# A two-layer attention kernel with every engine's order rewritten: small products set between long projections, group moments in three VectorE operations instead of two

## The chip, the cores and the metric

The kernel runs on one core of a Trainium2 chip. The metric is the device time of one execution in microseconds (us). The comparison is between the kernel before and the kernel with the change, each timed in several runs; one further execution of each is recorded by the hardware profiler.

## The reference

The input is 32 images of 16 x 16 positions with 256 channels, all float32. Two residual layers follow each other, each behind a group normalisation with 32 groups of 8 channels. Layer 0 is windowed attention (8 x 8 windows, shifted by 4, 16 heads, cosine similarity, a position bias, softmax). Layer 1 is linear attention along the columns and along the rows (no softmax), the two results added.

```python
def _gn(v, G=32, eps=1e-05):
    g = v.reshape(B_, H_, W_, G, C_ // G)
    m = jnp.mean(g, axis=(1, 2, 4), keepdims=True)
    s = jnp.var(g, axis=(1, 2, 4), keepdims=True)
    return ((g - m) / jnp.sqrt(s + eps)).reshape(v.shape)
# layer 0, on windows xw of the shifted image
q, k, v = xw @ Wq.T, xw @ Wk.T, xw @ Wv.T + bv
logits = (q / |q|) . (k / |k|) * scale + 16 * sigmoid(bias) + mask
z = softmax(logits) . v @ Wo.T + bo
# layer 1, for the columns and for the rows
q, k, v = split(x @ w_qkv, 3)
out = (q . k^T * d ** -0.5) . v @ w_out
x = x + layer0(_gn(x)); x = x + layer1(_gn(x))
```

## The kernel before, in words

**Work.** An image is held with channels on the 128 partitions, as two halves of 256 tokens. Each operand of a large product is split into a float16 high part and a float16 low part (the remainder), and a product takes three passes (PASSES). So each tensor that feeds TensorE costs a copy to float16 on ScalarE (`..._high`) and a subtraction for the remainder, on GpSimd (`..._low`: whole minus high, line L908) or on VectorE where the whole lies in PSUM.

**Staging.** The kernel is written by hand as five instruction streams, one per engine, and each stream is a loop over steps k. In step k a stream works on several images, each at another stage: `for img in there(k - 3): axial_kv(1, img)` means that in step k the row half of layer 1 makes keys and values of image k - 3. In full swing each step does all of the work of one image, so the length of a step times 32, and the ramps at both ends, is the time. Within a step the order is written out by hand; each engine runs its stream strictly in that order and waits on semaphores: `reach(engine, semaphore, img)` waits until that stage of that image is done (`earlier(img, 2)` is two images back, `earlier(img, -1)` one ahead); `edge(...)` is the same wait, written only for the first and the last 8 images.

**TensorE**, by stage: `window_qk` (24 products of 256 columns), `window_v` (12), `scores` (96 small ones), `window_pv` (64 small), `window_den` (16), `window_out` (12); `group_means` (a product of 12 columns that spreads the group sums, once per layer); `axial_kv` (12 of 512 columns, for a = 0 columns and a = 1 rows), `axial_q` (12), `gram_matmuls` (96 small), `axial_out` (32 pairs of small ones), `axial_y` (24), and transposes `image_channels`, `result_rows`.

**The chain that matters.** On VectorE `add_x` adds the residual, `group_stats` takes statistics of each half, `group_moments` turns them into mean and second moment (four numbers a partition), TensorE's `group_means` sums over the group, `group_var` makes the variance in four tiny operations, GpSimd's `rstd` raises to the power -0.5 (L913), and `group_norm` applies it. `gn_small[layer]` counts the tiny steps, GN_STEPS per image. On VectorE also: `cap_norms`, `spread_norms`, `scale_qk` (the query and key norms), `mask_k`, `add_bias` (two operations of 1024 elements, behind `scores`), `gram_low`, `q1_low`, `o1_sum`, and `turn_squares` and `sum_heads` behind ScalarE's `squares`. The lines in the profile are L1050 and L1052 for the moments, L1059 to L1066 for the variance, L1188 for `add_x`, L1098 for `o1_sum`.

**DMA.** Products of layer 1 are spread over partitions by DMAs from SyncE's queue (`spread_v_rows`, `spread_gram`).

**PSUM banks** are fixed per stage (QK_BANK and so on), so a stage that writes a bank waits for the reader of the stage that had it before.

## Time and profile before

| | us |
|---|---|
| three runs of the kernel before, median (lowest to highest) | 1011.24 (1006.41 to 1012.84) |
| profiled execution, device time | 1005.87 |
| its span in the profile | 1004.1 |
| TensorE busy (share of the span) | 862.2 (86%) |
| VectorE busy | 757.0 (75%) |
| ScalarE busy | 663.8 (66%) |
| GpSimd busy | 494.9 (49%) |
| mean granted TensorE clock, share of full | 0.963 |

The profiled execution lies 5.4 us under the median of the three runs. Busy time of TensorE counts overlapping small products once. L12 is line 12 of the kernel file, PE is TensorE (matmul), DVE is VectorE, ACT is ScalarE, POOL is GpSimd.

### The profile page before, as it was taken

To read this page: it belongs to the slowest core of one execution; us is meant where nothing else is said; L and a number is where in the kernel's file an instruction comes from. 1 tells how busy PE (TensorE), PEld (TensorE's weight loads), DVE (VectorE), ACT (ScalarE), POOL (GpSimd) and SP (SyncE) were. 2 spreads that over 40 slices of the span, in tenths; PEclk is the share of its full clock that TensorE was granted. 3 is DMA by queue.
4 is the path that set the end of the run, shared out by engine and by line. 5 is a ranking of instruction groups with operands and counts; after the bars stand their busy time and mean duration, and the time that the engine had idled before them with its cause. 6 is when DMAs were issued, how large, how long until landed. Compare 5 with 4: busy or idle time off the path is not lost.

```text
span 1004.1 us, 45923 instructions
## 1 busy us (share of the span) xinstructions
PE 862.2 (86%) x20128; PEld 662.0 (66%) x20128; DVE 757.0 (75%) x1493; ACT 663.8 (66%) x1106; POOL 494.9 (49%) x361
## 2 busy tenths in 40 slices
PE   2257899999999999889999989999999998999765
PEld 2244676777777776667777767777777776767554
DVE  3666888889888877788887777898888877797321
ACT  2336676777777777777666767777777776777441
POOL 5125455655555554645555546555555545544431
PEclk9777999999999999999999999999999999999887
DMA  5100333343333434343333343433333443333333
GB/s 167 32 12 17 73 75 72 72 86 72 69 78 71 79 79 85 80 85 67 71 71 74 78 84 80 86 73 71 74 78 73 83 83 80 74 66 66 65 76 74
DMA packets 334158, 74.04 MB, mean 74 GB/s; under 512 B 282356, under 2 KB 333446, under 8 KB 333958
## 3 DMA queue, kind: packets, MB, share of 16 engines
q1 hardware_dynamic: 333958, 71.11, 34.4%
q8 instruction: 158, 2.59, 1.1%
q14 instruction: 42, 0.34, 0.1%
HBM read 12.31 MB, written 8.40 MB: 21 GB/s over the span
## 4 chain that ended last, share of the span: by engine, by line
PE 55%; DVE 17%; issue 10%; ACT 9%; SPq 4%; POOL 2%; DMA 2%; ACTq 0%; POOLq 0%; DVEq 0%
PE ps L546 17%; PE ps L454 15%; DVE stat L1052 5%; PE ps L577 5%; ACT kv L717 3%; PE ps L592 3%; SPq L404 3%; PE ps L511 3%; PE ps L502 3%; DVE o L1098 3%; ACT v_diag L801 2%; PE ps L477 2%; PE ps L593 2%; PE ps L617 2%; PE ps L493 2%
## 5 line engine op out<-in xcount | busy, mean ns | idle before, releaser
L908 POOL TENSOR_TENSOR kv<-kv,kv 128x1024 f16<-128x1024 f32 x64 | 137.1, 2142 | 136.1 <-ACT kv L717 136.1
L908 POOL TENSOR_TENSOR xn<-xn,xn 128x512 f16<-128x512 f32 x64 | 74.4, 1162 | 122.4 <-ACT xn L754 122.4
L592 PE MATMUL ps<-q,gram_wide 128*128 128x32 f16 x2048 | 111.3, 176 | 6.1 <-DMA gram_wide<-gram 5.2
L577 PE MATMUL ps<-v_wide,kv 64*32 64x128 f16 x6144 | 73.8, 226 | 47.9 <-DVE o L1098 27.2
L1105 DVE STREAM_TRANSPOSE qk<-qk_sq 128x1024 f32<-128x1024 f32 x32 | 39.9, 1246 | 98.7 <-ACT qk_sq L772 98.7
L592 PEld LDWEIGHTS ps<-q,gram_wide 128*128 128x128 f16 x2048 | 108.7, 97 | 8.0 <-DMA gram_wide<-gram 5.8
L593 PE MATMUL ps<-q,gram_wide 128*128 128x16 f16 x2048 | 110.5, 169 | 0.0
L734 ACT ACTIVATE gram<-ps,small 128x512 f16<-128x512 f32 x128 | 94.8, 810 | 22.4 <-PE ps L577 22.4
L1092 DVE SCALAR_TENSOR_TENSOR gram<-ps,small,gram 128x512 f16<-128x512 f32 x128 | 93.5, 784 | 17.8 <-ACT gram L734 15.9
L593 PEld LDWEIGHTS ps<-q,gram_wide 128*128 128x128 f16 x2048 | 106.1, 97 | 0.7
L454 PE MATMUL ps<-xn,w_q 128*128 128x256 f16 x768 | 97.1, 276 | 6.8 <-POOL xn L908 4.5
L722 ACT ACTIVATE kv<-ps 128x1024 f32<-128x1024 f32 x64 | 65.5, 1024 | 53.8 <-PE ps L546 53.8
L577 PEld LDWEIGHTS ps<-v_wide,kv 64*32 64x32 f16 x6144 | 61.3, 91 | 55.9 <-issue 42.6
L604 PE MATMUL ps<-o,w_o 128*128 128x256 f16 x768 | 92.9, 280 | 3.2 <-POOL o L908 3.2
L546 PE MATMUL ps<-w_kv,xn_cols 128*128 128x512 f16 x384 | 92.1, 390 | 1.3 <-issue 1.1
L913 POOL TENSOR_TENSOR stat<-stat,small 128x2 f32<-128x2 f32 x64 | 52.0, 812 | 80.5 <-DVE stat L1066 79.3
L908 POOL TENSOR_TENSOR xn_cols<-xn,xn_cols 128x512 f16<-128x512 f32 x32 | 45.2, 1411 | 90.3 <-ACT xn_cols L760 90.3
L546 PE MATMUL ps<-w_kv,xn 128*128 128x512 f16 x384 | 89.0, 382 | 0.3 <-POOL xn L908 0.3
L604 PEld LDWEIGHTS ps<-o,w_o 128*128 128x128 f16 x768 | 76.9, 100 | 14.6 <-POOL o L908 4.0
L908 POOL TENSOR_TENSOR o<-o,o 128x512 f16<-128x512 f32 x64 | 74.3, 1161 | 23.2 <-ACT o L748 23.2
L908 POOL TENSOR_TENSOR qk<-qk 128x1024 f16<-128x1024 f32 x32 | 68.7, 2148 | 30.6 <-ACT qk L787 30.6
L454 PEld LDWEIGHTS ps<-xn,w_q 128*128 128x128 f16 x768 | 70.6, 99 | 19.2 <-issue 7.3
(119 smaller groups left out, 2003.2 us busy)
## 6 DMA issues: line engine op xcount, KB each, us to landing
gram_wide<-gram SPq DMA_DIRECT2D x256, 128.0 KB
v_wide<-kv SPq DMA_DIRECT2D x512, 32.0 KB, 2.0
x_in<-x SPq DMA_DIRECT2D x32, 128.0 KB
x_in<-x SPq DMA_DIRECT2D x64, 64.0 KB
out<-y_out SPq DMA_DIRECT2D x32, 128.0 KB
out<-y_out SPq DMA_DIRECT2D x64, 64.0 KB
probs<-L_conv_w_qkv SPq DMA_DIRECT2D x1, 768.0 KB, 4.9
x<-L_conv_w_qkv SPq DMA_DIRECT2D x1, 768.0 KB, 6.5
```

The lines of the kernel that those rows point to most:

```text
L454: last = pe.matmul(dst, w[:, wp, c, m * P:m * P + P], act[:, xp, c * TOK:(c + 1) * TOK], start=(n == 0), stop=(n == 5))
L546: last = pe.matmul(ps[:, KV_BANK[a] + t, :], xn1[a][:, xp, c * TOK + t * P:c * TOK + t * P + P], w_l1[a]["kv"][:, wp, c, :], start=(n == 0 ...
L577: last = pe.matmul(dst.rearrange("p (s e) -> p s e", e=32), kv[a][rows, kp, t, own], v_wide[a][rows, :, vp, t, own], start=(n == 0), stop= ...
L592: pe.matmul(dst.rearrange("p (t i) -> p t i", t=2), high, q1[a][:, :, cols], start=True, stop=False)
L593: last = pe.matmul(dst[:, 0:SEQ], low, q1[a][:, 0, cols], start=False, stop=True)
L604: last = pe.matmul(ps[:, Y_BANK, g * TOK:(g + 1) * TOK], w_l1[a]["o"][:, wp, c2, g * P:(g + 1) * P], o1[a][:, xp, c2 * TOK:(c2 + 1) * TOK] ...
L722: act.activation(kv32[a][:], ps[:, KV_BANK[a]:KV_BANK[a] + 2, :], ACT.Copy).then_inc(kv_copied[a], 1)
L734: last = act.activation(gram_half(a, head, 0), gram_psum(a, head), ACT.Copy, scale=gram_mask[:, head:head + 1])
L908: return pool.tensor_tensor(dst, whole, high, ALU.subtract)
L913: pool.tensor_tensor(stat[layer][:, 28:30], stat[layer][:, 26:28], minus_half, ALU.pow).then_inc(gn_pow[layer], 1)
L1052: dve.scalar_tensor_tensor(sq_sum, sq_sum, 2.0 / TOK, s[:, 12:16], ALU.mult, ALU.add).then_inc(done, 1)
L1092: last = dve.scalar_tensor_tensor(gram_half(a, head, 1), gram_psum(a, head), gram_mask[:, head:head + 1], gram_half(a, head, 0), ALU.mult, ...
```

## The change

All five streams get a new order, every PSUM bank is assigned anew, the waits follow from that, and some stages move to another step (TensorE's stream has 38 steps in place of 37). In `group_moments` the one operation that scaled the second moment and added the squared mean becomes a multiplication by a constant and an addition; GN_STEPS goes from 10 to 11. No product, copy or DMA is added or dropped.

```diff
-        GN_STEPS = 10
+        GN_STEPS = 11
...
-        QK_BANK, V_BANK, DEN_BANK, PV_BANK, Z_BANK, Y_BANK, YT_BANK, XT_BANK = 4, 7, 4, 3, 3, 3, 2, 2
-        S_BANK, KV_BANK, Q_BANK = (5, 3), (5, 6), (5, 2)
-        G_BANK, O_BANK, GM_BANK = (0, 0), (0, 3), (7, 2)
+        QK_BANK, V_BANK, DEN_BANK, PV_BANK, Z_BANK, Y_BANK, YT_BANK, XT_BANK = 6, 7, 1, 5, 0, 0, 0, 5
+        S_BANK, KV_BANK, Q_BANK = (2, 5), (1, 1), (7, 4)
+        G_BANK, O_BANK, GM_BANK = (3, 3), (5, 2), (1, 0)
...
             def scores(img):
-                reach(pe, o1_summed[1], earlier(img, 3))
-                edge(pe, k_masked, img)
+                reach(pe, o1_summed[0], earlier(img, 3))
+                edge(pe, kv_hi[1], earlier(img, 2))
...
             def axial_out(a, img):
                 reach(pe, gram_spread[a], img, 64)
                 if a == 0:
-                    edge(pe, gram_lo[1], img)
+                    reach(pe, xt_copied, earlier(img, -4))
                 else:
-                    reach(pe, y_added, earlier(img, 1))
+                    reach(pe, biased[0], earlier(img, -3))
+                    edge(pe, kv_hi[1], earlier(img, -1))
...
             def group_means(layer, img):
+                reach(pe, gn_small[layer], img, GN_STEPS, 5)
                 if layer == 0:
-                    reach(pe, v_ready, earlier(img, 1))
-                    edge(pe, gn_small[0], img, GN_STEPS, 4)
-                else:
-                    reach(pe, xt_copied, earlier(img, -2))
-                    reach(pe, gn_small[1], img, GN_STEPS, 4)
+                    reach(pe, kv_hi[1], earlier(img, 3))
...
             def group_moments(layer, img):
                 reach(dve, done, img, GN_STEPS, 2)
                 dve.tensor_tensor(s[:, 12:16], mean, mean, ALU.mult).then_inc(done, 1)
-                reach(dve, done, img, GN_STEPS, 3)
-                dve.scalar_tensor_tensor(sq_sum, sq_sum, 2.0 / TOK, s[:, 12:16], ALU.mult, ALU.add).then_inc(done, 1)
+                dve.tensor_scalar(sq_sum, sq_sum, 2.0 / TOK, None, ALU.mult).then_inc(done, 1)
+                reach(dve, done, img, GN_STEPS, 4)
+                dve.tensor_tensor(sq_sum, sq_sum, s[:, 12:16], ALU.add).then_inc(done, 1)
```

A whole step of TensorE's stream now reads: `window_v`, `group_means(1)`, `axial_out(0)`, `axial_q(1)`, `axial_q(0)`, `group_means(0)`, `scores`, `axial_y`, `axial_out(1)`, `window_pv`, `window_den`, `window_qk`, `result_rows`, `gram_matmuls(0)`, `axial_kv(0)`, `window_out`, `image_channels`, `gram_matmuls(1)`, `axial_kv(1)`.

The rows below are instructions in the order in which an engine runs them, with what each writes and reads, sizes, and a count of equal ones.

TensorE before, in the middle of the program, from the rows' gram products to the queries and keys of layer 0 (`kv` with `v_wide` is `gram_matmuls`, `qk` with `k_two` is `scores`):

```order
L577 MATMUL ps<-v_wide,kv 32x128 x96
L477 MATMUL ps<-w_v,xn 128x256 x12
L493 MATMUL ps<-qk,k_two 128x64 x96
L454 MATMUL ps<-xn,w_q 128x256 x12
L639 MATMUL ps<-stat,group 128x12
L577 MATMUL ps<-v_wide,kv 32x128 x96
L546 MATMUL ps<-w_kv,xn_cols 128x512 x12
L502 MATMUL ps<-probs,small 32x256 x8
L617 MATMUL ps<-ident,y 128x128 x4
L511 MATMUL ps<-probs,v_diag 32x64 x32
```

TensorE after, from the queries and keys of layer 0 to the group sum of layer 1 of the next step:

```order
L454 MATMUL ps<-xn,w_q 128x256 x12
L454 MATMUL ps<-xn,w_k 128x256 x12
L620 MATMUL ps<-ident,y 128x128 x4
L580 MATMUL ps<-v_wide,kv 32x128 x96
L548 MATMUL ps<-w_kv,xn_cols 128x512 x12
L454 MATMUL ps<-o,w_o 128x256 x12
L630 MATMUL ps<-ident,x_in 128x128 x4
L580 MATMUL ps<-v_wide,kv 32x128 x96
L548 MATMUL ps<-w_kv,xn 128x512 x12
L477 MATMUL ps<-w_v,xn 128x256 x12
L638 MATMUL ps<-stat,group 128x12
```

Three groups of small products stood within five rows; now each gram group has a long projection behind it, and layer 1's group sum stands right behind the values of layer 0.

VectorE before, behind the sum over heads; `x1` is the residual sum of layer 1's input:

```order
L1112 TENSOR_REDUCE head_sum<-qk32 128x64
L1188 TENSOR_TENSOR x1<-z,x_t 128x32x8 x2
L1123 SCALAR_TENSOR_TENSOR head_norm<-head_rnorm,head_scale 128x64
L1043 BN_STATS stat1<-x1 128x6 x2
L1129 STREAM_TRANSPOSE qk_sq<-head_norm 128x1024
L1050 TENSOR_TENSOR stat1<-stat1 128x4
L1052 SCALAR_TENSOR_TENSOR stat1<-stat1 128x4
L1135 TENSOR_TENSOR qk32<-qk_sq,ps 128x1024
```

VectorE after, at the same place:

```order
L1114 TENSOR_REDUCE head_sum<-qk32 128x64
L1094 SCALAR_TENSOR_TENSOR gram<-ps,small,gram 128x32x16 x2
L1125 SCALAR_TENSOR_TENSOR head_norm<-head_rnorm,head_scale 128x64
L1131 STREAM_TRANSPOSE qk_sq<-head_norm 128x1024
L1137 TENSOR_TENSOR qk32<-qk_sq,ps 128x1024
L1190 TENSOR_TENSOR x1<-z,x_t 128x32x8 x2
L1044 BN_STATS stat1<-x1 128x6 x2
L1051 TENSOR_TENSOR stat1<-stat1 128x4
L1052 TENSOR_SCALAR stat1<-stat1 128x4
L1054 TENSOR_TENSOR stat1<-stat1 128x4
L1094 SCALAR_TENSOR_TENSOR gram<-ps,small,gram 128x32x16 x2
```

The residual sum and the moments of layer 1 stood ahead of the scaling of queries and keys, and now stand behind it and behind one `gram_low`.

GpSimd before, the remainders around the normed queries and keys (`qk`):

```order
L908 TENSOR_TENSOR o<-o32,o 128x512
L908 TENSOR_TENSOR kv_0<-kv32_0,kv_0 128x1024
L908 TENSOR_TENSOR o1_1<-o1_32_1,o1_1 128x512
L908 TENSOR_TENSOR kv_1<-kv32_1,kv_1 128x1024
L908 TENSOR_TENSOR qk<-qk32,qk 128x2x512
L913 TENSOR_TENSOR stat1<-stat1,small 128x2
```

GpSimd after:

```order
L909 TENSOR_TENSOR o<-o32,o 128x512
L909 TENSOR_TENSOR kv_0<-kv32_0,kv_0 128x1024
L909 TENSOR_TENSOR o1_0<-o1_32_0,o1_0 128x512
L909 TENSOR_TENSOR qk<-qk32,qk 128x2x512
L909 TENSOR_TENSOR o1_1<-o1_32_1,o1_1 128x512
L914 TENSOR_TENSOR stat1<-stat1,small 128x2
L909 TENSOR_TENSOR kv_1<-kv32_1,kv_1 128x1024
L914 TENSOR_TENSOR stat0<-stat0,small 128x2
```

Both `o1` remainders now stand directly around that of `qk`, and the remainder of `kv_1` moved from ahead of the power of layer 1 to between the two powers.

## Rows read from the trace of the kernel before

**Rows 1.** The page, parts 1 and 2: busy time, and the granted clock

```profile
PE 862.2 (86%) x20128; PEld 662.0 (66%) x20128; DVE 757.0 (75%) x1493; ACT 663.8 (66%) x1106; POOL 494.9 (49%) x361
...
PEclk9777999999999999999999999999999999999887
```

**Rows 2.** The chain that ended last, columns' keys and values (start, length, what)

```profile
161.42 2.70 PE ps L546 x12
...
868.96 2.70 PE ps L546 x12
```

**Rows 3.** The same chain from 640 to 675 us

```profile
642.43 0.95 PE ps L577 x96
643.38 2.70 PE ps L546 x12
...
647.08 0.59 PE ps L617 x4
...
648.69 2.73 PE ps L454 x24
...
653.01 1.33 PE ps L454 x12
```

**Rows 4.** Waits, longest in total: who waited for whom, us, times, longest

```profile
PE ps L577 <- DVE o L1098: 27.2, 28, 1.1
...
PE ps L639 <- ACT v_diag L801: 11.1, 16, 2.0
...
PE ps L577 <- issue: 10.9, 14, 1.2
PE ps L493 <- issue: 9.8, 13, 1.0
```

**Rows 5.** VectorE in order of time, from 517.5 us

```profile
517.85 0.26 DVE L1050 TENSOR_TENSOR stat<-stat 128x4 f32<-128x4 f32 x1
518.14 2.07 DVE L1052 SCALAR_TENSOR_TENSOR stat<-stat 128x4 f32<-128x4 f32 x1
...
521.98 0.87 DVE L1145 TENSOR_SCALAR k_two<-qk,small 128x1024 f16<-128x1024 f16 x2
```

**Rows 6.** GpSimd in the same stretch

```profile
515.95 2.14 POOL L908 TENSOR_TENSOR kv<-kv,kv 128x1024 f16<-128x1024 f32 x1 [4.35 <-ACT kv L717]
518.04 2.15 POOL L908 TENSOR_TENSOR qk<-qk 128x1024 f16<-128x1024 f32 x1
521.56 0.94 POOL L913 TENSOR_TENSOR stat<-stat,small 128x2 f32<-128x2 f32 x1 [1.36 <-DVE stat L1066]
```

**Rows 7.** VectorE from 67 us, then TensorE from 66 us

```profile
70.56 0.16 DVE L1062 TENSOR_TENSOR stat<-stat 128x2 f32<-128x2 f32 x1
70.75 1.97 DVE L1064 TENSOR_TENSOR stat<-stat 128x2 f32<-128x2 f32 x1
...
73.78 1.47 PE L493 MATMUL ps<-qk,k_two 32*128 32x64 f16 x96 [3.16 <-DVE k_two L1145]
```

**Rows 8.** Groups by line: count, busy us, mean ns of one, idle before

```profile
L1092 DVE SCALAR_TENSOR_TENSOR gram<-ps,small,gram 128x512 f16<-128x512 f32 x128 | 93.5, 784 | 17.8 <-ACT gram L734 15.9
L1152 DVE TENSOR_TENSOR probs<-ps,bias_mask 128x1024 f32<-128x1024 f32 x64 | 75.2, 1218 | 5.2 <-PE ps L493 4.7
...
L1129 DVE STREAM_TRANSPOSE qk_sq<-head_norm 128x1024 f32<-128x1024 f32 x32 | 39.3, 1229 | 0.0
...
L1188 DVE TENSOR_TENSOR x<-z,x_t 128x256 f32<-128x256 f32 x64 | 24.4, 422 | 12.2 <-ACT z L824 12.2
```

**Rows 9.** The same view of ScalarE and of GpSimd

```profile
L717 ACT ACTIVATE kv<-ps 128x1024 f16<-128x1024 f32 x64 | 65.3, 1020 | 0.0
...
L908 POOL TENSOR_TENSOR kv<-kv,kv 128x1024 f16<-128x1024 f32 x64 | 137.1, 2142 | 136.1 <-ACT kv L717 136.1
...
L908 POOL TENSOR_TENSOR o<-o,o 128x512 f16<-128x512 f32 x64 | 74.3, 1161 | 23.2 <-ACT o L748 23.2
...
L913 POOL TENSOR_TENSOR stat<-stat,small 128x2 f32<-128x2 f32 x64 | 52.0, 812 | 80.5 <-DVE stat L1066 79.3 <-DVE stat L1064 1.2
```

More of the change, by code:

```diff
@@ L412, in step @@
             def step(k):
-                for img in there(k - 5):
+                for img in there(k - 6):
+                    spread_v_rows(0, img)
                     spread_v_rows(1, img)
@@ L643, in step @@
                 for img in there(k - 2):
+                    window_v(img)
+                for img in there(k - 3):
+                    group_means(1, img)
+                for img in there(k - 5):
+                    axial_out(0, img)
+                for img in there(k - 4):
+                    axial_q(1, img)
+                    axial_q(0, img)
+                for img in there(k - 1):
+                    group_means(0, img)
+                for img in there(k - 2):
+                    scores(img)
@@ new lines, in step @@
+                for img in there(k - 6):
+                    axial_y(img)
+                for img in there(k - 5):
+                    axial_out(1, img)
+                for img in there(k - 2):
+                    window_pv(img)
+                    window_den(img)
+                for img in there(k - 1):
+                    window_qk(img)
+                for img in there(k - 6):
+                    result_rows(img)
+                for img in there(k - 4):
+                    gram_matmuls(0, img)
@@ L651, in step @@
-                for img in there(k - 2):
-                    group_means(1, img)
-                for img in there(k - 3):
-                    axial_q(0, img)
-                for img in there(k - 4):
-                    axial_out(1, img)
-                for img in there(k - 3):
-                    gram_matmuls(0, img)
-                for img in there(k - 1):
-                    window_v(img)
-                    scores(img)
-                for img in there(k - 3):
-                    axial_q(1, img)
@@ L678, in step @@
-                for img in there(k - 3):
-                    axial_out(0, img)
-            over_steps(step, 6)
+            over_steps(step, 7)
         @block.scalar
@@ L960, in step @@
                     token_low(0, img)
-                for img in there(k - 4):
-                    o1_low(1, img)
-                for img in there(k - 2):
-                    token_low(1, img)
-            over_steps(step, 5)
+            over_steps(step, 6)
         @block.vector
@@ L1250, in step @@
                     sum_heads(img)
-                for img in there(k - 1):
-                    add_x(img)
+                for img in there(k - 3):
+                    gram_low(0, img)
             over_steps(step, 6)
```

186 lines of the change are left out of this document (90 added, 96 removed).

## The prediction

> **What bounds the kernel now.** I read the page first. TensorE is busy for 86% of the span, VectorE for 75%, the others less [rows 1]; the granted clock is at its full level (2.4 GHz) nearly everywhere between the ramps [rows 1]. So no engine is full, and the clock is not what is lost. The chain that ended last gives the length of a step: the columns' keys and values of one image begin at 161.42 us, those of the image 25 later at 868.96 us [rows 2], so a step takes (868.96 - 161.42)/25 = 28.3 us. The same chain gives what TensorE's groups cost when one follows the other: 2.70 us for twelve products of 512 columns, 1.33 for twelve of 256, 2.73 for twenty-four, 0.95 for a group of small ones, 0.59 for four transposes [rows 3]; the pairs of `axial_out` lie between 651.42 and 653.01, which is 1.6 us [rows 3].
>
> The waits tell what fills the rest. TensorE waited 28 times, 27.2 us in all, for `o1_sum` (L1098) ahead of the gram products, 16 times for the spread of v, and 14 and 13 times, 10.9 and 9.8 us, in the middle of gram and score products for nothing the profile can name ("issue") [rows 4]. The first is 0.97 us a step, the second 11.1/28 = 0.4 and the issue gaps 20.7/28 = 0.7 as means over the steps. Without them a step would take 28.3 - 0.97 - 0.4 - 0.7 = 26.2. From the other side, group by group [rows 3]: the stages of 256 columns (queries and keys 2.73, y 2.7, and v, out and two q at 1.33 to 1.4) make 10.8, keys and values 2 x 2.7 = 5.4, and the small ones (two grams, scores, spread of v, denominators at 1.0 or so each, two `axial_out` at 1.6, transposes and sums 1.3) 9.5: 25.7. I take the middle, **25.9 us**, as TensorE's floor.
>
> Why is `o1_sum` late? Ahead of it on VectorE stands L1052, an operation on four numbers a partition that takes 2.07 us [rows 5]. It ends at 520.21; GpSimd's remainder of qk, from 518.04, ends at 520.19 [rows 6]. L1050, just before it, began at 517.85 and ended at 518.11, when GpSimd's remainder of kv had ended at 518.09 [rows 5, 6]. So a VectorE operation with two SBUF inputs stands still while GpSimd subtracts, and slips through at the border between two GpSimd operations. It is not a matter of the fused form: a plain TENSOR_TENSOR on two numbers took 1.97 us in one place and 0.16 just before it [rows 7]. This **hold** is what I follow through the new order.
>
> **The change part by part.**
>
> *The moments as plain operations.* Unheld, one more tiny operation costs about 0.2 us with its semaphore, by the two operations of rows 7 (starts 0.19 apart). That is 0.4 us a step of VectorE, where it has room. The hold is not removed: the last of the three still has two SBUF inputs. For the middle one, a TENSOR_SCALAR, no row of before shows it behind a GpSimd subtraction, so its hold lies between 0 and the length of one such subtraction, 1.16 us [rows 9].
>
> The Trainium skill, in "SBUF — State Buffer", section on which operations grab the shared pair of ports, says that `tensor_scalar` can run in a mode that takes VectorE's second port too and is then blocked like the two-input form. By that rule the middle operation would be held as well, and the sum below would be the same to 0.2 us, as the third is held behind the same subtraction.
>
> *The issue gaps.* All lie inside small groups that stood three in five rows; with a long projection behind each they should go: -0.7 us a step, or nothing if they come from elsewhere. They would be hidden by the waits below in any case.
>
> The Trainium skill, in "Runtime: NRT & Kernel Launch", section on instruction fetch, holds that fetching is hidden since the sequencer dispatches slower than blocks arrive. By that the gaps are something else and stay, up to 0.7 us a step; the rows show only their place.
>
> *The wait for o1_sum.* The gram products no longer follow directly on it, -0.97 us a step; `scores` waits for it now, with one long step of distance. Gone too is the wait for the spread of v.
>
> *The new order, followed from the end of `window_qk` (time 0).* ScalarE squares (1024 elements, 1.02 as the copy of [rows 9]), VectorE turns and sums (each as long as the transposition of rows 8, 1.23) to 3.6; then one `gram_low` (2 x 0.78 overlapping, 1.4), `cap_norms` 0.2, `spread_norms` 1.23, `scale_qk` 1.2, all from [rows 8, 9] or by the like size there. `add_x` is ready to start at **7.55**. TensorE meanwhile does 0.6 + 1.0 + 2.7 and ends the columns' kv at 4.3 [rows 3]; ScalarE copies it twice, 2 x 1.02 [rows 9], to 6.3; GpSimd subtracts from 6.4 to **8.5** (2.14) [rows 9]. So the first `add_x`, two SBUF inputs, is held to 8.5 and reads on to 8.8. GpSimd's next, the remainder of o1_0, is ready and takes 8.8 to 9.95; the second `add_x` goes through at 10.2; the remainder of qk takes 10.2 to 12.35 (as in rows 6); statistics end at 11.0, the first moment operation is held to 12.35; the remainder of o1_1 runs to 13.5; the second and third moment operations end at **13.7**. Without any hold it would be 7.55 + 0.8 + 0.8 + 0.4 = 9.5.
>
> TensorE goes on from 4.15 with 1.33 + 0.45 + 1.0 + 2.6 + 1.42 and stands at `group_means(1)` at 10.95. That group sum needs the moments. Held, it starts at 13.9: **TensorE idles 2.9 us**. Unheld it would not wait (9.5 < 10.95). Behind it are queued `axial_out(0)`, both `axial_q`, `scores`, and so `add_bias`.
>
> *A second hold.* From the moments (call it M) VectorE goes through `gram_low`, statistics, `mask_k`, moments, `o1_sum`, `group_var(1)`: 1.4 + 0.7 + 0.8 + 0.4 + 0.6 + 0.7, to M + 4.4 (the shapes of [rows 5, 8], each start some 0.08 before the end of the one ahead; statistics taken as long as two `add_x`, `o1_sum` as half a `add_bias`, the variance as four of the 0.19 of rows 7). GpSimd then takes the power, 0.81 as a mean [rows 9] and 0.94 when VectorE's `k_two` overlaps it [rows 5, 6], and at M + 5.2 begins the remainder of kv_1, to M + 7.3. TensorE's group sum of layer 0 ends at M + 0.2 + 0.3 + 1.6 + 2 x 1.33 + 0.3 = M + 5.1, so the two-input operations of `group_var(0)` come at M + 5.3 to 5.5 and are held to M + 7.3. `add_bias` (2 x 1.22 [rows 8]) then ends at M + 9.9 and releases `axial_out(1)` (wait on `biased[0]`) at M + 10.0. TensorE is there at M + 4.9 + 0.95 + 2.65 = M + 8.5: **idle 1.5 us more**. The rest meets its times: the remainder of xn that `window_qk` needs comes some 0.4 us before it.
>
> *Sum.* 25.9 + 2.9 + 1.5 = 30.3 us a step, against 28.3: +2.0. Of the 38 steps some 26 are full and the others pay part; I count 27: +54 us. The ramps have one step more but an image passes 5.8 steps in place of 5.7: 0, give or take 10. Against the profiled execution, 1005.9 + 54 = **1060 us**; that execution lies 5.4 under the median of the runs, inside their spread, so the same number stands for the median.
>
> **The rivals.**
>
> *Half of the holds.* If `group_var(0)` gets through (its margin is 0.1 to 0.3 us, against a power of 0.7 or 0.95), the step is 25.9 + 2.9 = 28.8: 1005.9 + 0.5 x 27 = 1019. If the two `add_x` go through together and the middle moment is not held, the third ends at 12.4, the first idle time is 1.6 and the step 29.0: 1025; both together 27.5: 984. For: margins are small and each is read from one row. Together 985 to 1035.
>
> *No hold decides; TensorE bounds: faster.* This is the other side. If the `kv_0` subtraction ends before `add_x` comes, or `group_stats` lands in a free stretch, the moments are ready before 10.95 and the step falls to the floor, 25.9: 1005.9 - 2.4 x 27 = 941. It decides at 1.4 us of hold in all (10.95 - 9.5). For it: all other waits have slack, the issue gaps go. Against: the first overlap alone (7.55 inside 6.4 to 8.5) is 1 us long, and two more subtractions are queued right behind. 935 to 985.
>
> *The clock falls.* With 2.9 and 1.5 us of idle time a step TensorE may be granted half its clock (1.2 GHz) at times: in the ramp, where the clock row shows 7 [rows 1], the score group behind 3.16 us of idle time took 1.47 us [rows 7], where a group of 96 at full clock takes 0.95 [rows 3]. If a third of the steps ran their 8 us between the two waits so, about 3 us more each: +1 us a step, 1087; more often, 1110.
>
> *The issue gaps stay* where TensorE does not wait anyway: +0.3 a step, 1068, inside the forecast's own range.
>
> **How the numbers follow.** The forecast (both holds) 45%, own range 1035 to 1080; half of the holds 20%; TensorE-bound 20%; falling clock 12%; gaps stay 3%. The range must hold 8 in 10: from 962 (most of the TensorE-bound case left out, 17%) to 1100 (3%). Within 1% of 1011 is what a measurement of this kernel can hardly tell from no change: 1001 to 1021. Faster than that: the 20% and a quarter of the half-holds' 20%, 26%. Same: about 15%. Slower: 59%.
>
> **What would show it.** Right: the list of waits has TensorE waiting at the group sum (L638) for the last moment operation (L1054), near 2.9 us a time, and at `axial_out(1)` for `add_bias` (L1154); L1190 shows means far over 0.42 us, L1051, L1052 and L1054 over 0.2, L1064 or L1066 some 2 us in each step, each ending with a GpSimd row; issue gaps vanish from L580 and L493. Wrong: L1190 at 0.42 and the group sum unwaited. The forecast fails if a hold is not what it seems (the arbitration lets VectorE's pairs through), or if a chain through DMA (`gram_spread`, due 0.7 us before `axial_out(0)` in the TensorE-bound case) becomes the limit.

## The result, and the profile after

The changed kernel takes 1058.59 us as the median of four runs (1057.6 to 1061.35), the kernel before 1008.89 (1006.41 to 1012.84, four runs beside them, three of which are those of the table before): a ratio of 1.0516, 95% interval 1.0482 to 1.0551. The profiled execution of after has a span of 1057.1 us.

The page of after, parts 1, 2 and 4, against [rows 1, 2]:

```profile
PE 888.2 (84%) x20128; PEld 678.8 (64%) x20128; DVE 837.1 (79%) x1557; ACT 659.0 (62%) x1106; POOL 495.4 (47%) x361
...
PEclk8579889999999899999999999999999999899987
...
PE 46%; DVE 34%; issue 11%; ACT 5%; SPq 3%; DMA 1%; POOL 0%; DVEq 0%; POOLq 0%; ACTq 0%
```

The same instructions keep TensorE busy 26 us longer and VectorE 80 us longer. VectorE did not get 80 us of work: 64 small operations of 0.16 us are 10 us. Most of the rest is standing still: `add_x` (L1190) alone shows 78.2 us in place of 24.4. VectorE carries a third of the chain that ended last. The mean granted clock of the core is 0.914, before 0.963. With the two levels of 1 and 0.5 that is 2 x 0.086 x 1057.1 = 182 us at the lower level (1.2 GHz), against 2 x 0.037 x 1004.1 = 74 us before, most of that in the ramps.

The step can be read from the four transposes of `x_in`, which stand once in each. Here those of image 7 and image 31, with first and last start:

```profile
L630 PE MATMUL ps<-ident,x_in x4: 272/272/273, 209.0 to 209.3; 128*128 128x128 f32 x4
...
L630 PE MATMUL ps<-ident,x_in x4: 272/272/273, 926.4 to 926.8; 128*128 128x128 f32 x4
```

(926.4 - 209.0)/24 = **29.89 us** a step. Before, the same two stand at 202.6 and 882.3: 28.32. So the middle costs 24 x 1.57 = 38 us, the start up to image 7 another 6.4, and the end behind image 31 (130.6 us in place of 121.7) 8.9.

The waits of after (who waited for whom: us, times, longest), against [rows 4]:

```profile
PE ps L638 <- DVE stat L1054: 77.4, 35, 2.7
...
PE ps L596 <- issue: 8.1, 9, 2.7
...
PE ps L596 <- DVE probs L1154: 4.7, 11, 0.7
```

TensorE's wait for `o1_sum` is gone. In its place `group_means` waits 35 times, 2.2 us a time, for the last of the moments. The wait of `axial_out(1)` for `add_bias`, forecast at 1.5 us a step, is small: 4.7 us under that name, and in the 24 steps another 3.1 us of the L596 waits called "issue", which end 0.10 us behind the end of `add_bias` like the named ones (0.15). Together that is 0.3 us a step.

VectorE's groups by line, against [rows 8]: busy, then the mean of one in ns.

```profile
L1190 DVE TENSOR_TENSOR x<-z,x_t 128x256 f32<-128x256 f32 x64 | 78.2, 1260 | 3.6 <-ACT z L822 3.6
L1051 DVE TENSOR_TENSOR stat<-stat 128x4 f32<-128x4 f32 x64 | 41.7, 651 | 1.1
L1054 DVE TENSOR_TENSOR stat<-stat 128x4 f32<-128x4 f32 x64 | 33.9, 529 | 2.2
L1064 DVE TENSOR_TENSOR stat<-stat 128x2 f32<-128x2 f32 x64 | 29.7, 464 | 2.2
...
L1052 DVE TENSOR_SCALAR stat<-stat 128x4 f32<-128x4 f32 x64 | 10.3, 161 | 0.0
```

`add_x` (L1190) takes three times its 422 ns of before. One step in order of time shows why. `window_qk` ended at 500.13. VectorE, then GpSimd, from there on:

```profile
507.64 2.42 DVE L1190 TENSOR_TENSOR x<-z,x_t 128x256 f32<-128x256 f32 x2
...
510.89 1.18 DVE L1051 TENSOR_TENSOR stat<-stat 128x4 f32<-128x4 f32 x1
511.99 0.16 DVE L1052 TENSOR_SCALAR stat<-stat 128x4 f32<-128x4 f32 x1
512.18 1.00 DVE L1054 TENSOR_TENSOR stat<-stat 128x4 f32<-128x4 f32 x1
...
519.62 0.85 DVE L1064 TENSOR_TENSOR stat<-stat 128x2 f32<-128x2 f32 x1
...
520.82 2.36 DVE L1154 TENSOR_TENSOR probs<-ps,bias_mask 128x1024 f32<-128x1024 f32 x2
```

```profile
506.35 2.14 POOL L909 TENSOR_TENSOR kv<-kv,kv 128x1024 f16<-128x1024 f32 x1 [3.41 <-ACT kv L720]
508.44 1.34 POOL L909 TENSOR_TENSOR o<-o,o 128x512 f16<-128x512 f32 x1
509.75 2.30 POOL L909 TENSOR_TENSOR qk<-qk 128x1024 f16<-128x1024 f32 x1
512.01 1.15 POOL L909 TENSOR_TENSOR o<-o,o 128x512 f16<-128x512 f32 x1
...
518.33 2.13 POOL L909 TENSOR_TENSOR kv<-kv,kv 128x1024 f16<-128x1024 f32 x1
```

Each held operation ends with a GpSimd row: L1051 at 512.07 with qk at 512.05, L1054 at 513.18 with the second o at 513.16, L1064 at 520.47 with kv at 520.46. L1052 slips in at the border between two subtractions, as in every step: its 64 times are all 149 to 194 ns, and none had to start in the middle of a subtraction. TensorE in the same step, and what clock it was granted in four stretches (busy times and counts by engine, then the granted clock):

```profile
509.41 1.47 PE L477 MATMUL ps<-w_v,xn 128*128 128x256 f16 x12
513.24 0.39 PE L638 MATMUL ps<-stat,group 128*128 128x12 f32 x2 [2.35 <-DVE stat L1054]
```

```profile
512.00:514.50 2.50, 1.26 (x43) 1.26 (x44) 2.46 (x6) 1.17 (x4) 1.16 (x2) 1.00 0.00 0
514.50:517.90 3.40, 3.40 (x44) 2.59 (x41) 2.96 (x13) 1.51 (x2) 0.22 (x1) 0.50 0.47 81
517.90:520.00 2.10, 2.10 (x101) 1.96 (x100) 0.54 (x2) 0.60 (x1) 2.10 (x2) 0.99 0.79 143
```

TensorE is idle for 2.35 us, works on for 1.3 us, and is then at its lower level for 3.4 us. Of the 24 steps, 23 hold such a fall of the clock. The one that holds none, from 268.3 us, shows what the two holds do when TensorE keeps its speed:

```profile
281.36 2.05 DVE L1066 TENSOR_TENSOR stat<-stat 128x2 f32<-128x2 f32 x1
```

```profile
281.27 2.13 POOL L909 TENSOR_TENSOR kv<-kv,kv 128x1024 f16<-128x1024 f32 x1
```

```profile
286.01 0.18 PE L596 MATMUL ps<-q,gram_wide 128*128 128x32 f16 x1 [1.32 <-issue]
```

The group sum of layer 1 waits 2.35 us there too, the variance of layer 0 is held for 2.05 us, `add_bias` ends at 285.90, and `axial_out(1)` has waited 1.32 us when it starts 0.1 us behind that. The step takes 29.31 us.

### The profile page after: what moved, and what is told of

It reads as the page before. It is cut to its first block, busy times and chain, and to the rows that moved or that the text cites. A ratio compares the mean times of both kernels' runs of the same rounds, so it can differ in the third digit from the quotient of the medians.

```text
span 1057.1 us, 45985 instructions
## 1 busy us (share of the span) xinstructions
PE 888.2 (84%) x20128; PEld 678.8 (64%) x20128; DVE 837.1 (79%) x1557; ACT 659.0 (62%) x1106; POOL 495.4 (47%) x361
## 4 chain that ended last, share of the span: by engine, by line
PE 46%; DVE 34%; issue 11%; ACT 5%; SPq 3%; DMA 1%; POOL 0%; DVEq 0%; POOLq 0%; ACTq 0%
PE ps L454 20%; DVE x L1190 7%; PE ps L596 7%; PE ps L609 5%; DVE gram L1094 4%; DVE qk L1107 4%; DVE qk_sq L1131 4%; DVE stat L1051 3%; PE ps L511 3%; PE ps L597 3%; ACT qk_sq L770 3%; PE ps L501 3%; DVE stat L1054 3%; DVE stat L1044 2%; PE ps L493 2%
## 5 line engine op out<-in xcount | busy, mean ns | idle before, releaser
L454 PE MATMUL ps<-xn,w_q 128*128 128x256 f16 x768 | 126.3, 330 | 4.5 <-POOL xn L909 4.5
L596 PE MATMUL ps<-q,gram_wide 128*128 128x32 f16 x2048 | 112.9, 179 | 19.3 <-issue 8.1
L596 PEld LDWEIGHTS ps<-q,gram_wide 128*128 128x128 f16 x2048 | 111.2, 100 | 27.1 <-issue 20.2
L914 POOL TENSOR_TENSOR stat<-stat,small 128x2 f32<-128x2 f32 x64 | 44.1, 689 | 170.2 <-DVE stat L1068 170.2
L763 ACT ACTIVATE probs<-probs 128x1024 f32<-128x1024 f32 x64 | 67.7, 1058 | 80.3 <-DVE probs L1154 77.9
L454 PEld LDWEIGHTS ps<-xn,w_q 128*128 128x128 f16 x768 | 84.4, 116 | 39.0 <-issue 9.3
L597 PEld LDWEIGHTS ps<-q,gram_wide 128*128 128x128 f16 x2048 | 107.5, 98 | 0.1
L548 PE MATMUL ps<-w_kv,xn 128*128 128x512 f16 x384 | 88.4, 380 | 1.7 <-issue 1.4
L909 POOL TENSOR_TENSOR o<-o,o 128x512 f16<-128x512 f32 x64 | 79.2, 1239 | 22.7 <-ACT o L746 22.7
L548 PE MATMUL ps<-w_kv,xn_cols 128*128 128x512 f16 x384 | 88.4, 380 | 0.5 <-POOL xn_cols L909 0.5
L638 PE MATMUL ps<-stat,group 128*128 128x12 f32 x128 | 23.8, 260 | 77.4 <-DVE stat L1054 77.4
L909 POOL TENSOR_TENSOR qk<-qk 128x1024 f16<-128x1024 f32 x32 | 73.2, 2287 | 28.8 <-ACT qk L785 28.8
L725 ACT ACTIVATE q<-ps 128x512 f16<-128x512 f32 x64 | 37.6, 587 | 76.1 <-PE ps L454 73.9
L740 ACT ACTIVATE o<-ps 128x512 f32<-128x512 f32 x64 | 37.9, 592 | 73.3 <-PE ps L597 73.3
```

Of the source, the lines that this page charges most:

```text
L454: last = pe.matmul(dst, w[:, wp, c, m * P:m * P + P], act[:, xp, c * TOK:(c + 1) * TOK], start=(n == 0), stop=(n == 5))
L548: last = pe.matmul(ps[:, KV_BANK[a] + t, :], xn1[a][:, xp, c * TOK + t * P:c * TOK + t * P + P], w_l1[a]["kv"][:, wp, c, :], start=(n == 0 ...
L596: pe.matmul(dst.rearrange("p (t i) -> p t i", t=2), high, q1[a][:, :, cols], start=True, stop=False)
L597: last = pe.matmul(dst[:, 0:SEQ], low, q1[a][:, 0, cols], start=False, stop=True)
L763: act.activation(part, part, ACT.Exp).then_inc(probs_ready[g], 1)
L909: return pool.tensor_tensor(dst, whole, high, ALU.subtract)
```

## The experiments

Times are medians. Each kernel was timed against the kernel before on the same chip, and the ratio is to that. A step is read as above, from the transposes of `x_in`. "Early o1" and "late kv_1" name two moves in GpSimd's order; neither changes what is computed. A step "holds a fall" when the granted clock is at its lower level in some of it; "undisturbed" is a step without a fall and without a wait of TensorE of over a quarter of a us that is called "issue".

**1. The form of the moments, in both kernels.** In after, the two plain operations are fused again:

```
-dve.tensor_scalar(sq_sum, sq_sum, 2.0 / TOK, None, ALU.mult)
-dve.tensor_tensor(sq_sum, sq_sum, s[:, 12:16], ALU.add)
+dve.scalar_tensor_tensor(sq_sum, sq_sum, 2.0 / TOK, s[:, 12:16], ALU.mult, ALU.add)
```

> The changed kernel with the moments back as two operations (the fused one in place of the multiplication and the addition), order and banks as changed. Theory of the hold: the fused operation has two SBUF inputs and is held behind GpSimd's remainder of o1_1 exactly as the addition is, so the last moment of layer 1 ends at the same time: 1058 us, within 6, and L1052 shows about 1.0 us for layer 1. Rival, the form of the operation matters: if the split is what costs, -0.2 to -0.4 us a step, 1048 to 1053; if the fused form is slow by itself (2 us as in the profile of before), +1 us a step or more, 1085.

1054.82 us (1052.24 to 1062.09), ratio 1.0454 (1.0393 to 1.0515); step 29.79. The fused operation shows a mean of 564 ns where L1054 showed 529: it is held in the same place, and the time is inside the 1058 +- 6 of the theory.

The other way round, before with its fused operation split:

> The kernel before with the two fused moment operations (scalar_tensor_tensor) each written as a plain multiply and a plain add, its orders and banks as they were. What bears on the end of a step there is the wait of TensorE for o1_sum, about 1 us a step, which stands ahead of or behind this work. Theory (the form of the operations is worth next to nothing, the orders make the time): one small operation of about 0.16 us more per group of moments, at most 2 x 0.16 x 32 = 10 us if all of it lies on the path, 5 us if only that of one layer does; 1009 to 1015 us. Rival (the plain form brings or costs the time): over 1020 us, or under 1000 us.

1009.92 us against 1009.57, ratio 1.0005 (0.9981 to 1.0029). In the order before, the plain form is worth nothing, and in the new order the two intervals of the ratio overlap (1.0393 to 1.0515 and 1.0482 to 1.0551). So the 5% lies in the rest of the change: the orders, with the banks and waits that go with them.

**2. Before, with `o1_sum(0)` ahead of `group_moments(0)`**, so that TensorE's wait for it no longer hangs on a held operation:

```
+    for img in there(k - 4):
+        o1_sum(0, img)
     for img in there(k):
         group_moments(0, img)
-    for img in there(k - 4):
-        o1_sum(0, img)
```

> The kernel before with one swap on VectorE: o1_sum(0) ahead of group_moments(0), so that the sum for which TensorE waits 0.97 us a step no longer stands behind the held moment operation. Theory of the hold: that wait goes, 28.3 to 27.4 us a step, 1009 - 26 = 983 us; something else (the spread of v, the second gram wait) may take back half, 995. Rival, the wait is bounded by another chain (the held operation only shifts VectorE's later work, which sets the step): no change, 1009.

991.35 us, ratio 0.982 (0.9763 to 0.9876), step 27.81. Its groups on VectorE and waits of TensorE:

```profile
L1050 DVE TENSOR_TENSOR stat<-stat 128x4 f32<-128x4 f32 x64 | 53.2, 831 | 0.2
```

```profile
PE ps L639 <- ACT v_diag L801: 16.3, 23, 2.0
PE ps L493 <- DVE o L1098: 14.0, 19, 0.8
```

The hold has moved to L1050, and the sum for which TensorE waited ahead of the gram products (27.2 us before) does not stand behind it any more; a shorter wait for it, 14.0 us, is left ahead of the scores. The time is inside the theory's 983 to 995. The reading of [rows 5, 6] holds.

**3. After, with early o1.** GpSimd's remainders of o1_0 and o1_1 are taken from around `qk_low` and made ahead of `o_low`, one step of GpSimd's program earlier for the same image:

```
-    for img in there(k - 5):
-        o1_low(0, img)
     for img in there(k - 1):
         qk_low(img)
-    for img in there(k - 5):
-        o1_low(1, img)
...
+    for img in there(k - 4):
+        o1_low(0, img)
+        o1_low(1, img)
     for img in there(k - 1):
         o_low(img)
```

> The changed kernel with GpSimd's two remainders of o1 moved from around that of qk to ahead of that of o, into 3.1 us in which GpSimd is idle; nothing else. Theory of the hold: the second add_x is no longer held behind o1_0, the last moment no longer behind o1_1, so the moments of layer 1 end some 2.0 us earlier (11.1 us behind the queries and keys in place of 13.1), TensorE waits 0.4 us or less at the group sum in place of 2.35, and the step, which then follows the moments and the second hold (behind the remainder of kv_1, now 1.5 to 2 us), goes from 29.8 to 27.8: 1006 us, within 10. Rival, TensorE waits for the moments for another reason (VectorE simply late): no change, 1058.

1032.24 us (1030.45 to 1037.15), ratio 1.0227 (1.0173 to 1.028), step 29.15: in the right direction, and half of what was expected. The pause ahead of `group_means(1)` is 1.14 us, where 0.4 or less was expected, because the first moment operation is now held to the end of the remainder of qk. Two places of one step, VectorE and GpSimd:

```profile
622.22 1.53 DVE L1189 TENSOR_TENSOR x<-z,x_t 128x256 f32<-128x256 f32 x2
...
624.58 1.80 DVE L1050 TENSOR_TENSOR stat<-stat 128x4 f32<-128x4 f32 x1
...
631.90 2.05 DVE L1065 TENSOR_TENSOR stat<-stat 128x2 f32<-128x2 f32 x1
```

```profile
624.24 2.13 POOL L909 TENSOR_TENSOR qk<-qk 128x1024 f16<-128x1024 f32 x1 [1.10 <-ACT qk L785]
...
631.81 2.13 POOL L909 TENSOR_TENSOR kv<-kv,kv 128x1024 f16<-128x1024 f32 x1
```

`add_x` is down to 1.53 for the pair and the moments end 1.1 us earlier. With less waiting ahead, `group_var(0)` now runs fully into the remainder of kv_1, and `axial_out(1)` waits 1.3 to 1.5 us in 14 of the 24 steps: the second hold of the prediction, which the slow clock had covered in after. Twenty steps still hold a fall.

**4. After, with `window_v` computed twice** (12 products more per step, same result), to fill the pause ahead of `group_means(1)`:

```
-for t in range(2):
+for t in (0, 1, 0, 1):
```

> The changed kernel in which TensorE makes the values of layer 0 twice (12 more products of 256 columns, the same result into the same bank), 1.3 us of work placed in the 2.35 us for which it waits at the group sum of layer 1. The wait shrinks to about 1 us and the clock should stay at its full level there. Rival that counts the clock as its own cost (half the clock for 3.4 us a step, in which the two axial_q take 1.3 us longer): -1.0 to -1.3 us a step, 1024 to 1032. Theory of the two holds: the group sum of layer 0 then comes 1.3 us earlier, but its first two-input operation on VectorE stays held until GpSimd's remainder of kv_1 ends, so L1064 grows from 0.85 to about 2 us, add_bias starts when it did, and the time stays: 1058, within 8.

1073.57 us (1069.73 to 1081.7), ratio 1.0645 (1.0567 to 1.0722), outside what was expected. The pause is 0.97 us, as meant, but L1066 is held for 2.05 us, `axial_out(1)` waits 1.37 us, and in 14 of the 24 steps the clock falls right behind that wait:

```profile
437.00:440.70 3.70, 2.33 (x53) 1.97 (x52) 3.67 (x8) 2.19 (x3) 0.71 (x2) 1.00 0.18 43
440.80:444.20 3.40, 3.40 (x102) 2.87 (x102) 2.57 (x6) 3.40 (x7) 1.65 (x2) 0.50 0.18 44
```

There the products of the values and the denominators took 1.94 and 1.58 us in place of 1.10 and 1.05. The test mixed two things, so the second hold was taken out by itself.

**5. After, with late kv_1**: GpSimd's power of layer 0 ahead of `token_low(1)`:

```
+    for img in there(k):
+        rstd(0, img)
     for img in there(k - 3):
         token_low(1, img)
     for img in there(k):
-        rstd(0, img)
         normed_low(0, img)
```

> The changed kernel, with GpSimd's token_low(1) moved behind its rstd(0), so that its two subtractions no longer stand beside the DVE variance operations of group_var(0). Theory of the second hold: L1064 goes from 0.46 to about 0.16 us mean, add_bias starts about 0.8 us earlier in the steps in which the hold ended last. In the changed kernel the first axial product after it starts only 0.20 us per step late, the drop of the clock having taken up most of that slack, so that the gain is at most 0.3 us a step: 1045 to 1059 us, step 29.6 to 29.9. Rival (the second hold sets the step in full, 1.5 us a step as the prediction had it): step 28.4, 1010 to 1020 us. Rival of a cost: the later kv_1 delays the products of the values of layer 1, over 1065 us.

1051.03 us (1046.2 to 1057.74), ratio 1.0406 (1.0333 to 1.0479), step 29.54. The variance is not held at all now (L1065 shows 161 ns likewise):

```profile
L1067 DVE TENSOR_TENSOR stat<-stat 128x2 f32<-128x2 f32 x64 | 10.3, 162 | 2.2
```

Alone the second hold is worth 8 us, inside the theory's range; the step is just under its 29.6. Twenty of 24 steps hold a fall of the clock and take 29.75 us in the mean; the two undisturbed ones take 28.1.

**6. The same with `window_v` twice.** The first kernel meant for this went out without the second `window_v`. It is the kernel of experiment 5 a second time, and its expectation was not put to a test:

> The changed kernel with token_low(1) moved behind rstd(0), as in the run that gave 1051 us, and window_v written twice: its 12 products are computed a second time into the same bank with the same result, about 1.4 us more of work for TensorE in each step, ahead of group_means(1). The run without the second window_v had a step of 29.54 us, idle times of 2.25 us at group_means(1) and 0.03 us at the axial products, and TensorE at its lower level for 3.70 us a step. Theory (a pause of more than 2 us lets the clock fall, and that fall costs the rest: M = 13.05 us behind window_qk, plus 15.0 us of products behind it, makes 28.0 to 28.2 at the full clock): the added products fill the pause, 0.9 us of it are left, the clock stays at its higher level, and the step is 28.1 to 28.6, so 1008 to 1025 us, with more work and less time. Rival (the clock falls anyway, whatever the pause): step 29.5 to 30, 1050 to 1065 us.

1052.98 us, ratio 1.0383 (1.0339 to 1.0428): a repeat of experiment 5 within its interval. The kernel with the edit of experiment 4 in it:

> The changed kernel with token_low(1) behind rstd(0) and window_v written twice (12 products, the same result a second time, about 1.4 us more of work for TensorE in each step ahead of group_means(1)). The kernel without the second window_v gave 1051 and 1053 us, with steps of 29.54 and 29.61 us, a pause of 2.3 us at group_means(1) and 3.7 to 4.0 us a step at the lower clock. Theory (the length of that pause makes the clock fall, and without the fall the step is 13.05 + 15.0 = 28.0 to 28.2 us): the pause is 0.9 us, the clock stays up, step 28.1 to 28.6, 1008 to 1025 us: more work, less time. Rival (the clock falls whatever the pause, or what is saved there is lost at another pause): step 29.5 or more, 1050 us or more.

1029.5 us (1026.03 to 1031.59), ratio 1.0187 (1.0143 to 1.0232), step 28.85: in the direction of the theory, and outside its range (1008 to 1025). TensorE does 384 products more than in experiment 5 and the kernel is 22 us faster. Ten undisturbed steps take 27.99 us in the mean, as the theory had it; eight still hold a fall, such as this one, behind a pause of 0.88 us, and take 29.65:

```profile
501.00:503.80 2.80, 2.17 (x69) 2.14 (x70) 2.80 (x6) 1.44 (x5) 0.56 (x1) 1.00 0.00 0
503.82:507.23 3.41, 3.41 (x19) 2.35 (x17) 2.04 (x10) 1.35 (x2) 0.69 (x1) 0.50 0.91 151
```

So with the shorter pause the clock falls less often (20 steps of 24 before, 8 now), and each fall costs 1.7 us here; that a pause of 0.9 us ends all falls is wrong. The other six steps hold a gap of the kind called "issue".

**7. Both moves of GpSimd's work together** (experiments 3 and 5):

> The changed kernel with both moves of GpSimd's work: o1_low(0) and o1_low(1) behind qk_low, as in the run that gave 1032 us, and token_low(1) behind rstd(0). In that run the second hold (L1065 for 2.05 us) stood ahead of an idle time of 1.37 us at the first axial product of layer 1 and was what ended last in every second step. Theory (both holds are real and independent): that idle time goes too, the step falls from 29.15 to 28.0 +- 0.4, about 1002 us (990 to 1015), level with the kernel before. Rival (what is left is the clock at half and not the hold): within 8 us of 1032.

990.12 us (984.7 to 993.49), ratio 0.9796 (0.9741 to 0.9851), step 27.29. Alone the moves gave 26 and 8 us, together 68, and the result lies at the good end of the expected range; the step is under the 28.0 +- 0.4 of it. The clock's share is in the page and in the one wait that is left:

```profile
PEclk9778999999999999999999999999999999999987
```

```profile
PE ps L638 <- DVE stat L1054: 40.6, 33, 2.4
```

Five of 24 steps hold a fall (28.30 us in the mean), 14 are undisturbed (26.81). That the two moves give twice their sum goes with the clock: steps without a fall or an issue gap take 29.3 us in after (the one shown above), 28.2 to 28.3 in experiment 3 (two), 28.1 in experiment 5 (two) and 26.8 here, which is 1.1 and 1.2 us for the moves alone and 2.5 for both, nearly their sum; but 23, 20, 20 and 5 steps of 24 hold a fall.

**8. After, with moments of one input each.** The squares are made one by one with the mean as scalar operand, the sum as a reduction over pairs; GpSimd and all orders as in after (`mean_g` and `pairs` stand here for the views of single means and of pairs of columns):

```
-dve.tensor_tensor(s[:, 12:16], mean, mean, ALU.mult)
-dve.tensor_scalar(sq_sum, sq_sum, 2.0 / TOK, None, ALU.mult)
-dve.tensor_tensor(sq_sum, sq_sum, s[:, 12:16], ALU.add)
+for g in range(2 * G):
+    dve.tensor_scalar(s[:, 12 + 2*g : 13 + 2*g], mean_g, mean_g, None, ALU.mult)
+dve.tensor_scalar(s[:, 13:20:2], sq_sum, 2.0 / TOK, None, ALU.mult)
+dve.tensor_reduce(sq_sum, pairs(s[:, 12:20]), AXES.X, ALU.add)
```

> The changed kernel with the moments worked out by operations that have one input in SBUF each: the squares of the four means by four tensor_scalar operations with the mean as scalar operand, the sum by a tensor_reduce over pairs; same numbers, three operations more per image and layer. GpSimd and all orders as in the changed kernel. Theory (only VectorE operations with two inputs in SBUF stand still while GpSimd works): add_x is held as before (1.26 us mean), none of the moment operations is, M falls by 1.2 to 1.4 us (their 2.34 us become about 0.9), the idle time at group_means(1) from 2.3 to about 1.0 us; the hold of group_var(0) then sets the axial products, as in the run with the early o1_low: 1032 us, range 1022 to 1045. Rival (any small VectorE operation is held beside a GpSimd operation): one of the new ones shows 0.5 to 1 us mean and the time is 1055 to 1070.

1002.85 us (996.82 to 1009.51), ratio 0.9873 (0.9827 to 0.9919), step 28.01: 56 us faster than after, beyond the expected range. The lines show that the rule of the forecast, two SBUF inputs, was too simple:

```profile
L1052 DVE TENSOR_SCALAR stat<-stat 128x1 f32<-128x1 f32 x256 | 36.9, 209 | 1.2
L1055 DVE TENSOR_SCALAR stat<-stat 128x4 f32<-128x4 f32 x64 | 27.2, 425 | 0.0
...
L1057 DVE TENSOR_REDUCE stat<-stat 128x4 f32<-128x8 f32 x64 | 10.3, 161 | 2.2
```

L1055, one input, is held. Neither the squares nor the reduction are. L1055 has the form of the middle operation of after, but for its output, which steps by two columns and not three. With the moments earlier, `group_var(0)` also got through ahead of the remainder of kv_1 in most steps (L1068 at 290 ns mean): in one step its second subtraction ended at 470.32 and the remainder began at 470.49, which was luck and not in the theory. Thirteen undisturbed steps took 27.07 us, seven with a fall 29.49.

**9. The one-input moments on top of both moves:**

> The kernel with both moves of GpSimd's work (990 us, step 27.29, idle time of 1.04 us at group_means(1), L1051 held 0.90 us mean behind qk_low) and the moments by operations with one SBUF input each. Theory: nothing is held ahead of group_means(1) any more but little of add_x, the moments end about 0.9 us earlier, the idle time there falls to 0 to 0.2 us, and the step comes to 26.0 to 26.5, near TensorE's own 25.9: 952 to 970 us. Rival (something else ends just as late, the clock or an issue gap): the idle time is gone but the step stays above 27.0, 980 to 995 us.

989.44 us (987.41 to 991.43), ratio 0.9761 (0.9728 to 0.9793), step 27.42: no gain. The theory missed by 20 us. The time is in the rival's range, but not for its reason, since the pause ahead of `group_means(1)` is still 0.9 to 1.1 us. The hold had only changed its place, from L1051 to L1055. VectorE, then GpSimd:

```profile
428.10 0.58 DVE L1052 TENSOR_SCALAR stat<-stat 128x1 f32<-128x1 f32 x4
428.59 1.34 DVE L1055 TENSOR_SCALAR stat<-stat 128x4 f32<-128x4 f32 x1
429.96 0.16 DVE L1057 TENSOR_REDUCE stat<-stat 128x4 f32<-128x8 f32 x1
```

```profile
427.77 2.14 POOL L909 TENSOR_TENSOR qk<-qk 128x1024 f16<-128x1024 f32 x1 [1.11 <-ACT qk L785]
```

The squares ran inside the subtraction at their usual 0.58 for four, and L1055 ended 0.02 behind it, at 429.93.

**10. Both moves, and no holdable operation in the moments.** The factor 2/TOK goes into the variance, the squares are added behind TensorE's group sum:

```
+for g in range(2 * G):      # the only step ahead of group_means
+    dve.tensor_scalar(s[:, 3*g : 3*g + 1], mean_g, mean_g, TOK / 2.0, ALU.mult, ALU.mult)
...
+dve.tensor_reduce(s[:, 20:24:2], cols[:, :, 1:2], AXES.X, ALU.add)     # means, from PSUM
+dve.tensor_reduce(s[:, 21:24:2], cols[:, :, 0:3:2], AXES.XY, ALU.add)  # squares, from PSUM
+dve.scalar_tensor_tensor(s[:, 30:32], s[:, 21:24:2], 2.0 / TOK, s[:, 24:26], ALU.mult, ALU.subtract)
```

> The kernel with both moves of GpSimd's work (990 us, step 27.29, 1.04 us idle at group_means(1)), and the moments without any operation that a GpSimd operation was seen to hold. In the run with operations of one input the tensor_scalar on four strided elements still showed 0.67 us mean and ended with GpSimd's qk_low, while the squares (tensor_scalar on one element with an operand from SBUF, 256 of 256 at 0.2 us) and tensor_reduce (64 of 64 at 0.16 us) did not. Here only the four squares stand ahead of the sum over the channels; the factor 2/TOK and the addition of the squares are made behind it, by a second tensor_reduce from PSUM and in the subtraction of the variance. Same result but for rounding. Theory: the moments end about 0.75 us behind the statistics, 0.3 to 0.5 us ahead of TensorE, no idle time is left at group_means(1), the step is 25.9 to 26.4 and the time 945 to 965 us. Rival (something else ends just as late: issue gaps or the clock): step 26.8 to 27.3, 975 to 990 us.

**945.75 us** (941.07 to 948.14), ratio 0.9357 (0.9318 to 0.9396), at the good end of the range: the fastest of all, 6.4% under before and 10.7% under the changed kernel. Its page, its waits, and the squares inside GpSimd's subtraction:

```profile
PE 847.6 (90%) x20128; PEld 660.1 (70%) x20128; DVE 747.9 (79%) x1685; ACT 660.9 (70%) x1106; POOL 486.6 (52%) x361
...
PEclk9568999999999999999999999999999999999887
...
PE 68%; DVE 9%; SPq 9%; DMA 5%; issue 4%; ACT 3%; POOL 1%; POOLq 0%; DVEq 0%; ACTq 0%
```

```profile
PE ps L638 <- DVE stat L1051: 9.7, 6, 2.3
```

```profile
540.06 0.58 DVE L1051 TENSOR_SCALAR stat<-stat 128x1 f32<-128x1 f32 x4
```

```profile
539.66 2.13 POOL L909 TENSOR_TENSOR qk<-qk 128x1024 f16<-128x1024 f32 x1 [1.05 <-ACT qk L785]
```

TensorE is now what ends last. The group sum waits only in the ramps, no step between images 7 and 31 holds a fall, and a step takes 25.99 us; the 16 undisturbed ones take 25.63.

## Why the prediction was right, and where it was not

The time, 1060 against 1058.59, is closer than its terms deserve. Step by step:

**The floor, 25.9 us.** Right: experiment 10 has a step of 25.99, and 25.63 where nothing disturbs it.

**The first hold.** Right in mechanism, place and order. The sum had `add_x` done at 10.2, the moments at 13.7 us behind `window_qk` and TensorE at `group_means(1)` at 10.95. In the step shown they are 9.93, 13.05 and 10.75. So the pause is 2.35 us in place of 2.9. The 0.65 us of the moments is GpSimd's work being earlier: `kv` begins at 6.22 and not 6.4, the remainder of o1_0 follows at once, and that of qk begins at 9.62 and not 10.2. Experiments 3, 7, 8 and 10 show the cause, each by taking away some of what holds or of what can be held.

**The middle operation.** The forecast left its hold open, between 0 and 1.16 us, and named L1052 over 0.2 us as a sign; it shows 0.161, so that sign failed, without a cost to the sum. The reason is the place: it started at a border between two subtractions. Experiments 8 and 9 show that a `tensor_scalar` on four strided numbers with a constant is held like the others. The Trainium skill ("SBUF — State Buffer", section on who interferes with whom) says that `tensor_scalar` can take the shared ports and that `tensor_reduce` never contends on this chip. By that the trace agrees on both, and the forecast's "two SBUF inputs" was the narrower rule.

**The second hold.** Right as a hold, and the step of the sum that failed as a cost. It was to cost 1.5 us of idle time at `axial_out(1)`; in after it costs 0.3 us a step. Behind the end M of the moments the held part came as forecast: in the step shown the remainder of kv_1 ends at M + 7.28 (forecast 7.3) and `add_bias` at M + 10.0 (forecast 9.9). What was wrong is where TensorE stands by then. The sum had it at `axial_out(1)` at M + 8.5; it came at M + 9.8, since the clock had fallen and the two `axial_q` took 2.72 and 1.62 us in place of 1.47 each. The slow products filled the time of the wait. In the one step without a fall TensorE was there at M + 8.6 and waited 1.32 us, and this step is the forecast's mechanism whole: 25.6 + 2.35 + 1.32 = 29.3, measured 29.31. The rival of the falling clock named the other mechanism, gave it 12%, and added it to both holds; it came in place of the second. With the first hold at 2.3, 0.3 at `axial_out(1)`, 0.15 at issue gaps and about 1.5 for a fall (26.81 against 28.30 us in experiment 7, 27.99 against 29.65 in experiment 6), the step is 25.6 + 2.3 + 0.3 + 0.15 + 1.5 = 29.9, where the sum had 30.3. Against the 29.31 of the step without a fall, the falls cost the changed kernel no more than 0.4 to 0.5 us a step, since a fall takes the place of most of the second wait. Experiments 3 and 4 bring the second hold out at 1.4 us as soon as the first pause is shorter.

**The ramps.** They were put at 0, give or take 10. By the sum's own 27 full steps, 27 x 1.57 = 42.4 us of the measured 53.0 (1057.1 - 1004.1) lie in the steps, and 10.6 are left for the ramps. The step itself was put 0.43 us too long, which is 11.6 us over 27 steps. The two errors are of one size and of opposite signs, so the nearness of 1060 to 1058.59 is luck. The ramps' part was not tested by itself; it shrinks along with the holds (image 7 at 209.0 in after, 203.0 in experiment 7, 196.8 in experiment 10).

**The plain moments.** Right: nothing that the runs can tell (experiment 1).

**The issue gaps.** "Vanish from L580 and L493" is right for those lines in the stretch of the 24 steps. They appear at L511 and L501 instead (`window_pv` and `window_den`, which stand behind `axial_out(1)` with no long projection between), 0.15 us a step against 0.7 to 0.8 before. In other orders single ones lie elsewhere, such as 1.17 us inside a long projection (L548) in experiment 7, so what sets their place is not shown. The Trainium skill ("Runtime: NRT & Kernel Launch", section on instruction fetch) would have them be something else than fetching; no run here shows what they are.

**The rival on the other side** (nothing held, TensorE bounds, 941 us) was not what this kernel did, but its time was sound: experiment 10 makes that state, by another way, and takes 945.75.

**The chances.** "Faster" is given 26%, where its terms (20% and a quarter of 20%) give 25; nothing hangs on it.

Left open: what makes the clock fall behind one pause and not behind another like it. A pause of 2.2 to 2.6 us in nearly every step went with a fall in 18 to 23 of 24 steps (after, experiments 1 and 5), one of 0.9 to 1.2 us in 5 to 8 (experiments 6, 7, 9), one of 1.3 to 1.7 in 7 (experiment 8), none in none (experiment 10). But in experiment 3 all ten steps with a single pause of 1.0 to 1.2 us hold a fall, and so do 10 of the 14 that have the second pause as well; in experiment 4, with two pauses, 16 of 24 do. The length of one pause does not settle it.

## What to carry to other kernels

Before an order is changed, list which small VectorE operations stand on the path to TensorE, and lay GpSimd's rows over them; an operation of 0.16 us there can cost as much as the longest GpSimd operation. What paid here was to rewrite such an operation (one element with a scalar operand, a reduction, a constant folded in further on) and to move a GpSimd operation by one place; no run moved TensorE's groups back. And a pause of TensorE can be priced twice, once as idle time and once by the clock behind it, so that two savings can be worth twice their sum; test them together before dropping either. Where a second wait follows, the slow clock may only fill it, and then a step that kept its clock, if the trace has one, shows the holds by themselves.

## What the runs showed of the hardware that was not expected

A `tensor_scalar` on one number a partition with its scalar from SBUF was never held (256 of 256 between 192 and 247 ns in experiment 8, 120 of them wholly inside a GpSimd subtraction), while one on four strided numbers with a constant was, up to 1.34 us in the rows shown. GpSimd's power (L914, 0.69 us) held nothing: 41 two-input operations of the variance lie wholly inside one in experiment 8 and took 161 to 163 ns, so only the subtractions count as holders here. GpSimd pays too where it begins a subtraction while VectorE's `add_x` still runs: in after 30 subtractions of 512 elements took 1.34 us against 1.15 for the others, and 29 of the remainders of qk took 2.30 against 2.12. Adding 384 products to the kernel of experiment 5 made it 22 us faster, with 8 steps of 24 holding a fall of TensorE's clock in place of 20; adding them to the changed kernel, where the second hold was left, made it 15 us slower.
